# Routing of a transformer layer rebuilt: gate rows in three bf16 parts, tanh in place of exp, other PSUM banks, and another place for two table loads

## What is computed

```
x = layernorm(x + attention(x))                   # 16 heads share one key and one value head, causal
scores = x @ router_w.T                           # 8 experts
top, selected = top_k(scores, 2); top = softmax(top)
h = silu(x @ w1[e]) * (x @ w3[e])                 # bf16 products, 128 hidden units per expert
y = sum over the two selected e of top * (h @ w2[e])
x = layernorm(x + y)
```

## Time and profile before

| | |
|---|---|
| median of 3 runs | 1181.79 us (1181.24 to 1182.4) |
| the profiled execution | 1181.34 us, of it the profiled span 1179.2 us |
| granted TensorE clock, mean | 0.978 |
| busy share of the span | PE 93%, DVE 75%, ACT 60%, POOL 14% |

### The profile page before, as it was taken

One profiled execution on the slowest core, in us unless ns is written; L12 is line 12 of the kernel. 1 busy time (PEld: TensorE's weight loads), 2 busy tenths in 40 slices (PEclk: granted clock), 3 DMA queues, 4 the chain that ended last, 5 costly groups with the idle time before them and its releaser, 6 DMA issues.

```text
span 1179.2 us, 18318 instructions
## 1 busy us (share of the span) xinstructions
PE 1094.8 (93%) x6056; PEld 524.9 (45%) x6080; DVE 890.2 (75%) x1095; ACT 712.2 (60%) x828; POOL 165.4 (14%) x153
## 2 busy tenths in 40 slices
PE   5499999998999999999989998999999999999976
PEld 4146433743335543333734743374333564333442
DVE  3176688769888689889667767885988867988956
ACT  5354568337885477888327347844778546788811
POOL 2250121102001012001004103020200101200000
PEclk9599999999999999999999999999999999999998
DMA  3992540164001532000164164016210143200000
GB/s 125 206 150 67 117 103 1 37 144 108 1 1 38 112 104 36 2 2 1 45 136 110 45 135 108 1 38 143 86 23 1 37 87 94 36 1 1 2 2 36
DMA packets 65677, 74.36 MB, mean 63 GB/s; under 512 B 14224, under 2 KB 48016, under 8 KB 65552
## 3 DMA queue, kind: packets, MB, share of 16 engines
q1 hardware_dynamic: 49968, 58.74, 19.6%
q0 software_dynamic: 13584, 11.54, 6.6%
q10 hardware_dynamic: 2000, 2.51, 0.7%
HBM read 25.58 MB, written 8.39 MB: 29 GB/s over the span
## 4 chain that ended last, share of the span: by engine, by line
PE 70%; DVE 16%; issue 6%; POOL 2%; ACT 2%; SPq 2%; DMA 1%; DVEq 0%; ACTq 0%; POOLq 0%
PE sc L1059 18%; PE bank L1081 16%; PE sc L949 9%; DVE psum_k L749 8%; PE sc L1198 7%; PE bank L949 7%; PE sc L1213 2%; PE sc L1099 2%; SPq L364 2%; PE bank L1099 2%; POOL prob L460 2%; ACT prob L583 1%; DVE stats L825 1%; PE sc L1147 1%; PE bank L1206 1%
## 5 line engine op out<-in xcount | busy, mean ns | idle before, releaser
L583 ACT ACTIVATE prob<-sc 128x1024 f32<-128x1024 f32 x544 | 525.1, 1026 | 158.5 <-PE sc L1059 145.4
L749 DVE TENSOR_TENSOR psum_k<-psum_k,prob 128x2048 f32<-128x2048 f32 x170 | 395.6, 2327 | 5.1
L1059 PE MATMUL sc<-q_st,k_st 128*128 128x512 f32 x1088 | 334.9, 429 | 33.2 <-DMA q_st<-q_lo 13.1
L1059 PEld LDWEIGHTS sc<-q_st,k_st 128*128 128x128 f32 x1088 | 186.7, 191 | 280.8 <-ACT prob L583 178.0
L1081 PE MATMUL bank<-prob,v_sb 128*32 128x512 f32 x2176 | 290.2, 610 | 0.0
L460 POOL TENSOR_SCALAR_AFFINE_SELECT prob<-prob 128x1024 f32<-128x1024 f32 x64 | 88.0, 1410 | 596.0 <-ACT prob L583 596.0
L1198 PE MATMUL sc<-prob,w_sb 128*128 128x512 bf16 x488 | 117.5, 380 | 5.1 <-DVE prob L898 2.9
L749 DVE TENSOR_TENSOR psum_k<-prob 128x2048 f32<-128x2048 f32 x28 | 64.1, 2290 | 55.0 <-ACT prob L583 42.0
L1081 PEld LDWEIGHTS bank<-prob,v_sb 128*32 128x32 f32 x2176 | 44.0, 108 | 106.6 <-issue 90.8
L949 PE MATMUL bank<-q_st,wq_hi 128*128 128x512 f32 x240 | 80.8, 401 | 0.0
L615 ACT ACTIVATE prob<-sc 128x512 f32<-128x512 f32 x64 | 37.3, 597 | 68.1 <-PE sc L1198 68.0
(11 more groups left out here) (127 smaller groups left out, 1003.6 us busy)
## 6 DMA issues: line engine op xcount, KB each, us to landing
q_st<-q_hi SPq DMA_DIRECT2D x128, 128.0 KB, 2.7
q_st<-q_lo SPq DMA_DIRECT2D x128, 128.0 KB, 2.7
res<-in_x SPq DMA_DIRECT2D x8, 1024.0 KB, 5.1
res<-ob_sb POOLq DMA_DIRECT2D x8, 1024.0 KB, 8.1
out_x<-res SPq DMA_DIRECT2D x32, 256.0 KB, 2.5
res<-in_xT SPq DMA_DIRECT2D x7, 1024.0 KB, 5.3
w_sb<-in_w POOLq DMA_DIRECT2D x8, 256.0 KB, 10.9
prob<-in_wqkvT ACTq DMA_DIRECT2D x4, 288.0 KB, 5.8
```

The costliest lines, as they stand in the source:

```text
L583: nc.scalar.activation(prob[t % NP][:, half * HW:(half + 1) * HW], score_half(q // TB, 2 * t + half).rearrange("p m n -> p (m n)"), ACT.Ex ...
L749: nc.vector.tensor_tensor(acc[:, :], first[:, :], prob[t % NP][:, :], ALU.add).then_inc(add_v, 1)
L1059: last = nc.tensor.matmul(dst, k_st[:, k * P:(k + 1) * P], q_st[slot][:, c * HJ:(c + 1) * HJ, at:at + P], start=True, stop=not shift)
```

## The change

The routing chain and what stands around it:

- `ghl` holds three bf16 parts of each gate (24 columns per token) where it held two parts (16 columns, float32). The turn, `gT`, `pick` and `gate_rows` are bf16; the three parts add up to the float32 value.
- The two weights come from tanh, by two instructions that do not wait for each other, where there were three that did.
- The folded scores go into `top[0]` and the squares' sums into `top[1]`, so that `LOW[4]` and `LOW[5]` are free for expert 2.
- `times_linear` of expert 0 moves ahead of the routing steps on DVE, and silu of expert 0 ahead of `etop` on ACT. PE computes experts 2 and 3 before it turns `ghl`; `turn_norms` moves between them; `top_of_norms` moves behind the product of expert 1.
- The silu table is loaded by a one-element activation behind the last split of the context, the exp table by one behind the last silu of the block.
- Once, at the start, POOL makes a bf16 identity and a third selector stripe.

```diff
                 def finish(g):
-                    act.wait_ge(dtop_ready, count(b, dtop_ready, g + 1))
-                    nc.scalar.activation(etop[:, :], dtop[:, :], ACT.Exp).then_inc(etop_ready, 1)
                     for e in range(E):
                         act.wait_ge(up_done, count(b, up_done, E * g + e + 1))
                         if e >= 4:
                             act.wait_ge(prod_done, count(b, prod_done, E * g + e - 3))
                         nc.scalar.activation(silu[e % 4], LOW[2 * (e % 3)], ACT.Silu).then_inc(silu_done, 1)
+                        if e == 0:
+                            act.wait_ge(dtop_ready, count(b, dtop_ready, g + 1))
+                            nc.scalar.activation(etop[:, :], dtop[:, :], ACT.Tanh, scale=0.5).then_inc(etop_ready, 1)
                         if e == 2:
                             act.wait_ge(gates_turned, count(b, gates_turned, g + 1))
-                            nc.scalar.activation(gT[0:2 * E, :], top[0][0:2 * E, :], ACT.Copy).then_inc(gT_ready, 1)
+                            nc.scalar.activation(gT[0:3 * E, :], gates_bank(), ACT.Copy).then_inc(gT_ready, 1)
...
                     split_high_context(g, TB - 1)
+                    nc.scalar.activation(warm[:, 1:2], warm[:, 0:1], ACT.Silu)
...
                     finish(g)
+                    nc.scalar.activation(warm[:, 1:2], warm[:, 0:1], ACT.Exp)
...
                 def route(g):
                     dve.wait_ge(part_done, count(b, part_done, g + 1))
                     nc.vector.tensor_copy(rpart[:, :], top[0][:, :]).then_inc(rpart_ready, 1)
+                    times_linear(g, 0)
                     dve.wait_ge(routed, count(b, routed, g + 1))
...
                     dve.wait_ge(etop_ready, count(b, etop_ready, g + 1))
-                    step(nc.vector.tensor_scalar(den2[:, :], etop[:, :], 1.0, None, ALU.add))
-                    step(nc.vector.reciprocal(wtop[:, :, 0], den2[:, :]))
-                    step(nc.vector.tensor_tensor(wtop[:, :, 1], etop[:, :], wtop[:, :, 0], ALU.mult))
+                    nc.vector.tensor_scalar(wtop[:, :, 0], etop[:, :], -0.5, 0.5, ALU.mult, ALU.add)
+                    nc.vector.tensor_scalar(wtop[:, :, 1], etop[:, :], 0.5, 0.5, ALU.mult, ALU.add)
...
-                    step(nc.vector.tensor_copy(ghl[:, :, 0:E].bitcast(F32R), gate[:, :, :]))
-                    nc.vector.tensor_tensor(ghl[:, :, E:2 * E], gate[:, :, :], ghl[:, :, 0:E],
+                    step(nc.vector.tensor_copy(ghl[:, :, 0:E], gate[:, :, :]))
+                    step(nc.vector.tensor_tensor(grest[:, :, :], gate[:, :, :], ghl[:, :, 0:E], ALU.subtract))
+                    step(nc.vector.tensor_copy(ghl[:, :, E:2 * E], grest[:, :, :]))
+                    nc.vector.tensor_tensor(ghl[:, :, 2 * E:3 * E], grest[:, :, :], ghl[:, :, E:2 * E],
                                             ALU.subtract).then_inc(ghl_ready, 1)
...
                     with if_more(pe, b, g):
-                        pe.wait_ge(v_ready, count(b, v_ready, g + 2))
+                        pe.wait_ge(low_out, count(b, low_out, 5 * (g + 2)))
+                        pe.sem_inc(waited_apart, 1)
                         sum_squares(b, g + 1)
...
                 def experts(g):
-                    for e in range(1, 3):
-                        if e == 2:
-                            pe.wait_ge(dtop_ready, count(b, dtop_ready, g + 1))
-                            with if_more(pe, b, g):
-                                turn_norms(b, g + 1)
-                        up(g, e)
+                    up(g, 1)
+                    with if_more(pe, b, g):
+                        pe.wait_ge(v_ready, count(b, v_ready, g + 2))
+                        pe.sem_inc(waited_apart, 1)
+                    up(g, 2)
+                    with if_more(pe, b, g):
+                        turn_norms(b, g + 1)
+                    up(g, 3)
                     pe.wait_ge(ghl_ready, count(b, ghl_ready, g + 1))
                     for t in range(TB):
-                        last = nc.tensor.transpose(top[0][0:2 * E, t * P:(t + 1) * P], ghl[:, t, :], ident[:, :])
+                        last = nc.tensor.transpose(gates_bank()[:, t * P:(t + 1) * P], ghl[:, t, :], ident_b[:, :])
                     last.then_inc(gates_turned, 1)
-                    up(g, 3)
                     pe.wait_ge(gT_ready, count(b, gT_ready, g + 1))
```

More of the change, by code:

```diff
@@ L137, in build @@
         mhalf = sb("mhalf", [P, TB])
-        pick = sb("pick", [P, E], F32R)
+        pick = sb("pick", [P, E], BF16)
+        ident_b = sb("ident_b", [P, P], BF16)
         q_hi = sb("q_hi", [P, HJ, BT], F32R)
@@ L173, in build @@
         etop = sb("etop", [P, TB])
-        den2 = sb("den2", [P, TB])
+        warm = sb("warm", [P, 2])
         wtop = sb("wtop", [P, TB, 2])
@@ L177, in build @@
         gate = sb("gate", [P, TB, E])
-        ghl = sb("ghl", [P, TB, 2 * E])
-        gT = sb("gT", [P, BT], F32R)
+        ghl = sb("ghl", [P, TB, 3 * E], BF16)
+        grest = sb("grest", [P, TB, E])
+        gT = sb("gT", [P, BT], BF16)
         pick_f = prob[1][:, 0:E]
@@ L327, in gate_bank, with gates_bank @@
             return top[(e + 1) % 2]
+        def gates_bank():
+            return top[0][0:3 * E, 0:BT // 2].bitcast(BF16)
         def q_bank(g, j):
@@ L340, in den_bank, with squares_bank @@
             return sc[:, RING_AT[g]["den", q] % 3, 0, :] if q % TB < TB - 1 else top[0][:, :]
+        def squares_bank(g):
+            return LOW[5] if g == 0 else top[1]
         def down_bank(g, t):
@@ L423, in _ @@
             step(nc.gpsimd.memset(pick_f, 0.0))
-            for off in (0, E):
+            for off in (0, E, 2 * E):
                 step(nc.gpsimd.affine_select(out=pick_f, in_=pick_f, compare_op=ALU.not_equal,
@@ L427, in _ @@
                                              channel_multiplier=1))
+            step(nc.gpsimd.memset(ident_b[:, :], 0.0))
+            step(nc.gpsimd.affine_select(out=ident_b[:, :], in_=ident_b[:, :], compare_op=ALU.not_equal, fill=1.0,
+                                         base=0, pattern=[[-1, P]], channel_multiplier=1))
             for e in range(E):
@@ L513, in _ @@
             act.wait_ge(rT_cleared, 1)
-            nc.scalar.activation(etop[:, :], rT_sb[:, 0, E:E + TB], ACT.Copy)
+            nc.scalar.activation(warm[:, :], rT_sb[:, 0, E:E + 2], ACT.Copy)
             for c in range(DC):
@@ L858, in finish_attention, with times_linear @@
                         split_low_q(b, g + 1, 3)
+                def times_linear(g, e):
+                    dve.wait_ge(silu_done, count(b, silu_done, E * g + e + 1))
+                    nc.vector.tensor_tensor(prod[e % 4], LOW[2 * (e % 3) + 1], silu[e % 4], ALU.mult).then_inc(prod_done, 1)
                 def route(g):
@@ L862, in route @@
                     nc.vector.tensor_copy(rpart[:, :], top[0][:, :]).then_inc(rpart_ready, 1)
+                    times_linear(g, 0)
                     dve.wait_ge(routed, count(b, routed, g + 1))
-                    step(nc.vector.tensor_copy(rsc[:, :, :], LOW[4][:, 0:TB * E].rearrange("p (t e) -> p t e", t=TB)))
+                    step(nc.vector.tensor_copy(rsc[:, :, :], top[0][:, 0:TB * E].rearrange("p (t e) -> p t e", t=TB)))
                     for t in range(TB):
@@ L992, in sum_squares @@
                         at = t * H + j * HC
-                        nc.tensor.matmul(LOW[5][:, at:at + HC], squares[:, j, toks], head_pick[:, :],
+                        nc.tensor.matmul(squares_bank(g)[:, at:at + HC], squares[:, j, toks], head_pick[:, :],
                                          start=True, stop=True)
                     for n in range(2):
-                        last = nc.tensor.matmul(LOW[5][:, TB * H + t:TB * H + t + 1], squares_kv[:, n, toks],
+                        last = nc.tensor.matmul(squares_bank(g)[:, TB * H + t:TB * H + t + 1], squares_kv[:, n, toks],
                                                 ones_b[:, :], start=(n == 0), stop=(n == 1))
@@ L1188, in route @@
                     for t in range(TB):
-                        last = nc.tensor.matmul(LOW[4][:, t * E:(t + 1) * E], rpart[:, t * P:(t + 1) * P],
+                        last = nc.tensor.matmul(top[0][:, t * E:(t + 1) * E], rpart[:, t * P:(t + 1) * P],
                                                 fold_sel[:, :], start=True, stop=True)
@@ L1254, in _ @@
                 finish_experts(NG - 1)
-V_STEPS = NG * (2 * TB + 11)
+V_STEPS = NG * (2 * TB + 10)
 def max_steps(g):
```

13 lines of the change are left out of this document (5 added, 8 removed).

## The result

| | before | changed |
|---|---|---|
| median | 1182.1 us (1181.24 to 1183.94) | 1168.48 us (1166.44 to 1172.56) |
| profiled span | 1179.2 us | 1166.8 us (execution 1168.54 us) |
| granted clock, mean | 0.978 | 0.977 |

What follows compares the result with a forecast made beforehand. PE was taken as the bound, with 70% of the chain and idle pieces in routing. Gains of 10.1 + 1.6 = 11.7 us from 1181.34 gave 1169.6, plus 0.45 for the median: 1170.0 us, range 1164.5 to 1177.

Steps and rivals of the forecast that it cites:

- Stretches of 12.2 us, alike in seven blocks, one hole released by the copy: Sign: routing product to expert 4 takes about 12.2 us, with some 0.9 us hole before gate rows, ended by ACT's copy.
- The gain of the routing, 10.1 us: Routing product to expert 4: 1.1 to 1.6 us gained in each of seven blocks, 0.9 in the last; sum 10.1.
- 0.2 per block from expert 4 to the scores: Expert 4 to next scores: cheaper bf16 gate rows and earlier first `hT` save 0.2 us per block, 1.6 in all.
- Slack of 0.4 ahead of the turn: Routing, block one: `ghl` ready at 120.25, PE at its turn at 120.65, so 0.4 us of slack covers DVE's chain.
- Product 0 early, no wait at expert 3: Routing: DVE's product of expert 0 stands ahead of the scores, so PE's expert 3 loses its 0.36 us wait.
- Table loads at nothing: ACT's moved silu load (1.28 us) costs nothing, as ACT idled there for PE; no gain counted for the exp load.
- The tanh switch: Form of the late gate rows rival: tanh outside silu's set needs extra loads around `etop`; under 0.2 us per block.
- The rival that the exponentials carry: Attention's start hangs on ACT, so six blocks gain the load's 1.28 us on top: 7.7 us, 1162.3 us; chance 8%.
- The residual's wait for PE unchanged: Sign, next block's attention: DVE's 2.91 us wait before the residual, read as for PE's down products, stays the same.
- The clock: Rival: the new 0.9 us hole drops PE's clock in each block, costing 14.4 us against 11.7: 1184.5 us; chance 4%.
- Gate rows late: Rival, routing: DVE's chain or the copy costs 0.7 us more per block, 5.6 us less gain: 1175.6 us; chance 13%.
- the gain absorbed: Rival: next attention waits for something fixed, like a query transfer; only last block's 0.9 + 0.2 stays: 1180.7 us; chance 6%.

Runs made afterwards that it cites:

- Experiment 4: Two kernels against the changed one: three more dependent DVE steps in the routing chain, 1178.26 us; two float32 gate parts, float32 turn and gate rows, 1175.74 us.
- experiment 2: Changed kernel with DVE's product of expert 0 back behind the routing steps, ahead of that of expert 1: 1188.87 us.
- experiment 1: Two kernels against the changed one: exp table load back ahead of a block's first exponential, 1170.18 us; silu load back directly ahead of silu 0, 1169.56 us.
- experiments 3: Changed kernel with PE's turn of the gates ahead of expert 3 again, as before the change: 1178.8 us.
- the kernel with TensorE's order alone: Changed kernel with expert 4 between turn and gate rows on PE, later gate rows one expert later, DVE's order unchanged: 1176.34 us.

## Why the prediction held, point by point

Predicted 1170.0, measured 1168.48.

- *Stretches of 12.2 us, alike in seven blocks, one hole released by the copy.* It is 11.98 in six, 12.21 in the seventh, and the hole is where it was put. Of the stretch, `ghl` was foreseen 10.05 us after the routing product and came at 9.87, the turn 10.45 and 10.39, and the two gate rows 0.45 and 0.43. `ghl` was 0.18 early mostly because the two steps that do not wait for each other cost 0.05 (118.91 to 118.96) where 0.2 was taken; that only added slack. On PE's way the one term off by more than 0.1 is that from the turn to the copy: 0.64 was taken from the float32 turn, 0.43 was measured. Experiment 4 shows that this is the turn's type, as it is 0.63 again with float32. Over-priced by 0.2 per block.
- *The gain of the routing, 10.1 us.* By the two sets of stretches: 1.32, 1.62, 1.52, 1.59 in the first sequence, 1.3, 1.6, 1.5 in the second, and -0.54 in the last block, 10.0 in all. Two errors cancel: seven blocks gave 0.2 more each, and the last lost 0.5 instead of gaining 0.9. Its mechanism was right (10.89 at full clock, a gain of 1.0); what failed is that I priced it as if its clock were sure. A clock below 1.00 in these stretches was one of the signs of being wrong, and it showed in this one block. That the sum came out at 10 is luck in so far.
- *0.2 per block from expert 4 to the scores.* It is 0.35 in the first block, 0.2 to 0.5 in the six that lead to scores of the same sequence, and nothing in the fourth: 2.1 us in all for the 1.6. To the last `hT` it is 0.2 in each of the eight.
- *Slack of 0.4 ahead of the turn.* 0.52 in the first block, 0.1 to 0.25 in the next three, confirmed by experiment 4, whose 0.99 us cost 0.5 to 0.8.
- *Product 0 early, no wait at expert 3.* Right, and experiment 2 prices it at 18 to 20 us, of which some 3 are half clock; that is more than the whole change.
- *Table loads at nothing.* Right for both. The tanh switch, and the time near 1178 that the prediction drew from it, didn't come: with the table set loaded for silu, tanh ran without a load. The rival that the exponentials carry is refuted by experiment 1: they start 2.4 us earlier, as foreseen, and nobody uses it.
- *The residual's wait for PE unchanged.* The step that failed. I read the 2.91 us of the earlier trace rows as a wait for PE and drew from it that everything in the attention shifts by PE's gain. It is DVE's guard. PE's next scores came 1.6 us earlier, the residual only 1.2 (26.9 before, 25.7 now, in this block). The time held because the guard, too, starts when DVE has finished the previous block, which PE's gain brought forward; had DVE not moved, the gain would have ended here.
- *The clock.* In the changed kernel no fall stands at the new hole, in any block, so the rival falls as a forecast. It is real, though: with longer waits in the routing it came in two blocks in experiment 2 and in the last block in experiments 3 and 4.
- *Gate rows late, and the gain absorbed.* Neither came: the gate rows stand at 11.55, 0.2 earlier than laid out, and the next routing products come earlier by about what the stretches gave, or more.

The profile accounts for the 12.4 us of the span so: 10.0 in the stretches, 2.1 up to the next scores, 1.15 lost because the first block starts at 111.35 instead of 110.20, 1.3 in the attentions, where the moved falls of the clock are (1.0 and 1.2 gained, twice 0.4 lost), and 0.2 behind the last block's expert 4. The start is by chance (it was 109.62 with the silu load back). What stays open: without the branch the attention's adds begin 1.1 to 1.5 us earlier, but the next routing comes between 0.2 later and 1.3 earlier, and the returned falls of the clock explain this for blocks two and six only. For the kernel with TensorE's order alone, the last `hT` explains some 5 of the 6 to 8 us lost; the rest isn't settled. Nor is it what makes the clock fall in one attention and not in the next.

## What to carry to other kernels

Lay an order out in absolute times before it runs, and ask of each moved step which buffer it frees and for whom: the one product moved ahead of a chain was worth more than all the rest, and the same TensorE order without DVE's lost. Before you build on an idle time, compare its end with the end of the releaser that is named beside it; where the releaser had long been done, look into the waiting engine's own branches and register loads. A filled hole is a gain only if the work that it pushes back has slack where it lands.

## What the runs showed of the hardware

- Behind a guard's branch over a long fallback VectorE stood idle for 2.8 to 3.4 us, and for 3.2 to 3.7 with the guard in the other place; behind a branch over short code it took 0.15. The profile put the idle time down to a semaphore that had long been there, or to "issue".
- A turn of 24 bf16 rows lets the reader start 0.43 us after it begins, one of 16 float32 rows 0.63; the 0.59 us of the copy are alike.
- Tanh between silus needs no table load; a load of 1.28 us directly ahead of silu 0 cost nothing where ACT would have waited for PE.
- An idle piece of PE of 2.19 us was followed by half clock in one kernel and not in the other, and one of 4.46 us by half clock for 3.4 us in some runs, 6.8 and 10.2 in others. With product 0 late, waits of 1.81 to 2.13 us stood in all eight routings, and half clock followed in two of them. In the last block's routing two pieces of 0.97 and 0.94 with a turn between them were followed by half clock; 0.23 and 0.93, with the silu load back, were not.
